# Two expert layers around a state-space mixer: first-pass results scattered plainly to two row arrays and summed by VectorE in the mixer

## The reference

```
x = x + 0.5 * ffn(layernorm(x), Wg, W11, W12, W2)
x = x + mixer(layernorm(x))
x = x + 0.5 * ffn(layernorm(x), Wg, W11, W12, W2)

ffn(x):   s = softmax(x @ Wg)                  # 8 experts
          top 2 of s, their scores divided by their sum
          y_e = (silu(x @ W11[e]) * (x @ W12[e])) @ W2[e]      # 256 -> 512 -> 256
          out = sum over the two chosen e of score_e * y_e
mixer(T): Tn = T / rms(T) * norm_scale;  x, z = split(Tn @ in_w.T + in_b)
          x = pointwise(depthwise conv of 3 taps(x))
          y = (ssm forward(x) + ssm backward(x)) * sigmoid(z)  # h = h*a + u*b, 64 states each
          out = T + y @ out_w.T + out_b
```

## Time and profile before

| | us |
|---|---|
| median of 3 runs | 1028.68 (1026.73 to 1032.29) |
| the profiled execution | 1028.27, span 1026.4 |
| TensorE busy | 914.3 (89%) |
| VectorE busy | 591.1 (58%) |
| ScalarE busy | 340.2 (33%) |
| GpSimd busy | 607.3 (59%) |

### The profile page before, as it was taken

One profiled execution on the slowest core, in us unless ns is written; L12 is line 12 of the kernel. 1 busy time (PEld: TensorE's weight loads), 2 busy tenths in 40 slices (PEclk: granted clock), 3 DMA queues, 4 the chain that ended last, 5 costly groups with the idle time before them and its releaser, 6 DMA issues.

```text
span 1026.4 us, 20394 instructions
## 1 busy us (share of the span) xinstructions
PE 914.3 (89%) x5386; PEld 780.3 (76%) x5390; DVE 591.1 (58%) x1447; ACT 340.2 (33%) x699; POOL 607.3 (59%) x549
## 2 busy tenths in 40 slices
PE   7658899999999899976997994699999999999995
PEld 7647787878878788864774773478888888888884
DVE  3765565556656565546766875855555555555552
ACT  5743342333423333311327531023322332233221
POOL 3415666767667677734305760167777777777673
PEclk9969999999999999998999995699999999999999
DMA  9576547365363654323212548133344333433332
GB/s 315 195 264 187 150 89 195 77 168 160 79 188 73 179 131 95 49 32 103 63 41 86 186 156 347 45 71 77 53 74 77 56 72 53 79 76 52 52 50 30
DMA packets 78275, 116.06 MB, mean 113 GB/s; under 512 B 12048, under 2 KB 61072, under 8 KB 77904
## 3 DMA queue, kind: packets, MB, share of 16 engines
q0 software_dynamic: 31808, 37.83, 23.1%
q1 hardware_dynamic: 32896, 51.92, 14.8%
q10 hardware_dynamic: 13520, 25.70, 7.3%
HBM read 70.99 MB, written 48.63 MB: 117 GB/s over the span
## 4 chain that ended last, share of the span: by engine, by line
PE 60%; DVE 11%; issue 8%; POOL 6%; ACT 5%; DMA 4%; ACTq 3%; SPq 2%; POOLq 0%; another core or an unknown queue 0%; DVEq 0%
PE bank L1412 32%; PE bank L1435 16%; PE bank L1421 5%; PE bank L1404 3%; POOL seq L466 2%; PE bank L1533 2%; DVE work L834 2%; DMA xg<-xn_rows,idx_i 1%; SPq L306 1%; DVE sg L1078 1%; ACTq L648 1%; DVE bnst L822 1%; ACTq L646 1%; DVE w_lo L1143 1%; ACT sg L657 1%
## 5 line engine op out<-in xcount | busy, mean ns | idle before, releaser
L1078 DVE TENSOR_TENSOR sg<-sg,bank 128x512 f32<-128x512 f32 x142 | 97.7, 688 | 309.0 <-ACT sg L657 256.9
L1412 PE MATMUL bank<-w_hi,xt_hi 128*128 x568 | 241.3, 425 | 25.3 <-DVE xt_lo L1067 19.0
L1412 PE MATMUL bank<-w_hi,xt_lo 128*128 x568 | 224.6, 395 | 0.0
L1412 PE MATMUL bank<-w_lo,xt_hi 128*128 x568 | 222.8, 392 | 0.0
L649 ACT ACTIVATE yb<-bank,gates_in 128x256 f32<-128x256 f32 x142 | 67.4, 475 | 454.1 <-issue 234.0
L477 POOL DMA_INDIRECT xg<-xn_rows,idx_i x142 | 142.6, 1004 | 98.4 <-DVE idx_i L921 55.8
L481 POOL DMA_INDIRECT gates_in<-gate_rows,idx_g x142 | 138.6, 976 | 55.3 <-issue 42.3
L1435 PE MATMUL bank<-w_hi,ft_hi 128*128 x568 | 160.0, 282 | 7.7 <-ACT yb L649 7.7
L490 POOL DMA_INDIRECT x_rows<-yb,idx_i x71 | 116.5, 1641 | 82.5 <-ACT yb L649 30.5
L1435 PE MATMUL bank<-w_hi,ft_lo 128*128 x568 | 160.5, 283 | 0.0
L1435 PE MATMUL bank<-w_lo,ft_hi 128*128 x568 | 159.0, 280 | 0.0
(11 more groups left out here) (250 smaller groups left out, 1251.5 us busy)
## 6 DMA issues: line engine op xcount, KB each, us to landing
xn_rows<-work SPq DMA_DIRECT2D x16, 512.0 KB, 3.0
w_lo_rows<-w_lo ACTq DMA_DIRECT2D x16, 512.0 KB
w_lo<-w_lo_rows SPq DMA_DIRECT2D x16, 512.0 KB
work<-x_rows SPq DMA_DIRECT2D x16, 512.0 KB, 3.8
w_lo<-w_lo_rows SPq DMA_DIRECT2D x2, 4096.0 KB, 17.5
x_all<-x SPq DMA_DIRECT2D x8, 512.0 KB, 9.3
w_lo_rows<-in_sb ACTq DMA_DIRECT2D x16, 256.0 KB
out_rows<-seq SPq DMA_DIRECT2D x8, 512.0 KB, 3.3
```

Source lines behind the costliest of these rows:

```text
L1078: nc.vector.tensor_tensor(sg[p], sg[p], ps_g[p][:], ALU.mult).then_inc(f_step, 1)
L1412: last = nc.tensor.matmul(dst[p][:], xt[p][:, c, :], of(w), start=(c == 0 and n == 0), stop=(c == DC - 1 and n == len(parts) - 1))
```

## The change

The first pass no longer adds its results to a copy of x. Its index has one number per pair: first choices go to rows 0 to 4095 of a new array `y_rows`, second choices to rows 4096 to 8191, pads behind, by a plain scatter. The mixer loads x and both halves of y per chunk, VectorE adds them, and SP stores the sum to `x1_rows`. `norm_x1` moves from VectorE to ScalarE. SP, not ScalarE, loads the weights (a slot at a time, W2 directly into the place of its high part, from where ScalarE copies it to a stage) and stores the low parts of W11 and W12. The rounding of weights is cut into halves, one per tile. `apply_x` of chunks 0 to 3 moves to VectorE, with three buffers. GpSimd gathers six tiles' rows before the third gate gather. In the backward half the residual x + layernorm(x) is one ScalarE operation per tile, (1+rstd)*x - mean*rstd.

```
 SP, router:
-            for dram in (xn_dram, x1_dram, out):
+            for dram in (xn_dram, out):
...
-                sp.wait_ge(norm_ready, k + 1)
-                sp.dma_start(rows(xn_dram, k), xn[k % 2]).then_inc(xn_out[k % 2], 16)
-            sp.dma_start(x1_dram[0:L, :].rearrange(...), x.rearrange(...)).then_inc(x1_out, 16)
+                sp.dma_start(rows(xn_dram, k), xn_x[k % 3]).then_inc(xn_x_out[k % 3], 16)
 SP, first pass (a new order; load_slot loads w11, w12, then w2 of slot j):
             store_gates(0)
-            load_w2_lo(0)
+            load_w2_lo(0, 0)
+            def load_ahead(j, tile):
+                sp.wait_ge(ye_done, tile + 1)
+                load_slot(sp, j)
+            load_ahead(1, 1)
+            store_up_lo(0)
+            load_ahead(2, 5)
+            load_w2_lo(0, 1)
+            load_ahead(3, 9)
+            store_up_lo(1)
+            load_ahead(4, 13)
...
 SP, mixer:
-            sp.wait_ge(added, 16 * ET)
-            for b in range(2):
-                sp.dma_start(xin[b], rows(x1_dram, b)).then_inc(x_in[b], 16)
...
+            for p in range(2):
+                sp.wait_ge(y_out[p], 16 * ((ET + 1 - p) // 2))
+            sp.wait_ge(lo_out, 32 * E)
+            load_x1(0, 0)
+            load_y(0)
+            load_x1(1, 1)
+            for i in range(NCH):
+                b = i % 2
+                sp.wait_ge(summed, i + 1)
+                if i + 1 < NCH:
+                    load_y(i + 1)
+                sp.dma_start(rows(x1_dram, i), xin[b]).then_inc(x1_out[b], 16)
+                if i + 2 < NCH:
+                    sp.wait_ge(norm_ready, i + 1)
+                    sp.wait_ge(x1_out[b], 16 * (i // 2 + 1))
+                    load_x1(i + 2, b)
 GpSimd, experts:
+                    if r == 0:
+                        nc.gpsimd.indirect_dma_start(y_dram, bass.IndirectOffsetOnAxis(ap=idx_s[:, t:t + 1], axis=0), yb[t % 2], None).then_inc(y_out[t % 2], 16)
+                        return
...
-                for t in range(XG):
+                for t in range(XG + 1):
                     gather(t)
                 pool.wait_ge(gates_out, 16 * (r + 1))
                 for t in range(XG):
                     gather_gates(t)
+                    if t == 1:
+                        gather(XG + 1)
 GpSimd, residual:
-                nc.gpsimd.tensor_tensor(x2[b], xin[b], t_rows[b], ALU.add).then_inc(res_step, 1)
-                nc.gpsimd.tensor_tensor(x2[b], x2[b], outb_sb[:]..., ALU.add).then_inc(res_ready, 1)
+                nc.gpsimd.tensor_tensor(x2[b], t_rows[b], outb_sb[:]..., ALU.add).then_inc(res_ready, 1)
 ScalarE, weights:
+            def high_down(j, h):
+                at_ = w2_hi[:, j * IC + 2 * h:j * IC + 2 * h + 2, :].rearrange("p c d -> p (c d)")
+                act.wait_ge(w2_in, 16 * (j + 1))
+                if j > 0:
+                    act.wait_ge(w2_lo_out, 16 * j)
+                nc.scalar.activation(w2_stage[h], at_.bitcast(F32), ACT.Copy).then_inc(staged, 1)
+                act.wait_ge(staged, 2 * j + h + 1)
+                nc.scalar.activation(at_, w2_stage[h], ACT.Copy).then_inc(hi2_ready, 1)
 in weights_step:
+                    if s in (1, 2):
+                        high_down(j, s - 1)
                     if s == 4:
                         store_low(j)            # now one DMA, of w2's low part
+                    if s in (3, 4):
+                        high_up(j, s - 3)
+                    if s in (5, 6):
+                        high_value(j, s - 5)
 ScalarE, router:
-                if k > 0:
-                    apply_x(k - 1, (k - 1) % 2)
-            apply_x(NCH - 1, (NCH - 1) % 2)
+                if k > NCH // 2:
+                    apply_x(k - 1)              # apply_x(7) follows the first one-hot product
 ScalarE, mixer:
+            def norm_x1(i, b):
+                act.wait_ge(rstd_ready, i + (NCH + 1))
+                if not (isinstance(i, int) and i < 2):
+                    act.wait_ge(tr_done, i - 1)
+                for t in range(G):
+                    last = nc.scalar.activation(xn[b][:, t, :], xin[b][:, t, :], ACT.Identity, scale=rstd[:, b, 1, t:t + 1], bias=rstd[:, b, 0, t:t + 1])
+                last.then_inc(norm_ready, 1)
             for i in range(2):
-                rows_high(i, i)
+                norm_x1(i, i)
+            rows_high(0, 0)
+            rows_high(1, 1)
+            norm_x1(2, 0)
             gate_out(0)
-            with act.Fori(0, NCH // 2 - 1) as j:
+            norm_x1(3, 1)
+            with act.Fori(0, NCH // 2 - 2) as j:
                 for b in range(2):
                     rows_high(j * 2 + (b + 2), b)
                     gate_out(j * 2 + (b + 1))
+                    norm_x1(j * 2 + (b + 4), b)
 VectorE, router, after top2_x(k):
+                if 3 <= k < 7:
+                    apply_x(k - 3)
 VectorE, mixer:
             def stats_x1(i, m, b):
                 dve.wait_ge(x_in[b], m * 16 + 16)
+                dve.wait_ge(y_in, i * 32 + 32)
+                flat = xin[b].rearrange("p t d -> p (t d)")
+                nc.vector.tensor_tensor(flat, flat, y_in_sb[0], ALU.add).then_inc(half_sum, 1)
+                dve.wait_ge(half_sum, i + 1)
+                nc.vector.tensor_tensor(flat, flat, y_in_sb[1], ALU.add).then_inc(summed, 1)
+                dve.wait_ge(summed, i + 1)
                 ln_stats(i + NCH, b, rows_of(b))
...
             with dve.Fori(0, NCH // 2 - 2) as j:
                 for b in range(2):
                     c = j * 2 + b
-                    norm_x1(j * 2 + (b + 3), 1 - b)
                     take_u(c, b)
                     rows_low(j * 2 + (b + 2), b)
                     scan_forward(c)
                     stats_x1(j * 2 + (b + 4), j + 2, b)
```

More of the change, by code:

```diff
@@ new lines, in _ @@
+            load_ahead(1, 1)
[5 more added lines that the diff above has]
+            load_ahead(4, 13)
+            load_w2_lo(0, 2)
+            store_up_lo(2)
+            load_ahead(5, 16)
+            load_ahead(6, 19)
+            load_ahead(7, 22)
+            for j in range(3, E):
+                load_w2_lo(0, j)
+                store_up_lo(j)
+            sp.wait_ge(w2_lo_in, E * 16)
@@ L518, in _ @@
             experts(0)
-            with pool.Fori(0, NCH // 2) as j:
-                for b in range(2):
-                    rsqrt_rms(j * 2 + b, b)
+            for i in range(NCH):
+                rsqrt_rms(i, i % 2)
             pool.wait_ge(s_attw, 64)
@@ L573, in high_value @@
+            def high_value(j, c):
                 act.wait_ge(w12_in, 16 * (j + 1))
[L574 to L581 removed]
@@ L626, in tiles_by_p @@
                     nc.scalar.activation(pair_tile_x[g % 2][:, 0], at_tile[g % 2], ACT.Copy, scale=p_plus_1[:]).then_inc(by_p_ready, 1)
+                    if g == 0:
+                        apply_x(NCH - 1)
+                    if g == NQB - 1:
+                        act.wait_ge(xn_x_out[2], 16 * (NCH // 3))
                     if g > 0:
-                        (high_up, high_value, high_down)[g - 1](0)
+                        for c in range(2):
+                            (high_up, high_value, high_down)[g - 1](0, c)
             def experts(r):
@@ L729, in _ @@
                     gate_out(j * 2 + (b + 1))
+                    norm_x1(j * 2 + (b + 4), b)
+            for i in range(NCH - 2, NCH):
+                rows_high(i, i % 2)
+                gate_out(i - 1)
             gate_out(NCH - 1)
@@ L828, in ln_stats, with apply_x @@
                 last.then_inc(mv_ready, 1)
+            def apply_x(k):
+                dve.wait_ge(rstd_ready, k + 1)
+                if k >= 3:
+                    dve.wait_ge(xn_x_out[k % 3], 16 * (k // 3))
+                for t in range(k * G, (k + 1) * G):
+                    last = nc.vector.tensor_scalar(xn_x[k % 3][:, t % G, :], x_all[:, t, :], x1_rstd[:, t:t + 1], x1_mean[:, t:t + 1], ALU.mult, ALU.add)
+                last.then_inc(norm_dve, 1)
             def ln_apply(k, b, src, which=0):
@@ L1095, in experts @@
                     nc.vector.tensor_copy(v(UB), ps_w[:, D:D + 1]).then_inc(wct_ready, 1)
-                    low_down(0)
+                    for h in range(2):
+                        low_down(0, h)
                     gates(0)
@@ L1199, in _ @@
                 stats_x1(b, 0, b)
-            for b in range(2):
-                norm_x1(b, b)
             dve.wait_ge(m_ready, 1)
@@ L1205, in _ @@
             stats_x1(2, 1, 0)
-            norm_x1(2, 0)
             rows_low(1, 1)
```

316 lines of the change are left out of this document (162 added, 154 removed).

## The result

The changed kernel took 1092.19 us (median; 1091.62 to 1092.79), the kernel before beside it 1029.18 (1026.73 to 1032.29): ratio 1.0611 [1.0581, 1.064], slower. The profiled execution took 1091.62 with a span of 1089.9. The forecast was 1053, range 1033 to 1067: the direction was right, the size outside the range.

| stage | before | after | difference | forecast |
|---|---|---|---|---|
| to the first up product | 73.2 | 66.7 | -6.5 | -6.5 |
| first pass, to the last down product | 381.8 | 418.0 | **+36.2** | +1 (+11.5 -10.5) |
| to the last gate product of the mixer | 88.2 | 121.1 | +32.9 | +33 |
| to the last logits product | 81.6 | 78.6 | -3.0 | -3 |
| router, to the next up product | 37.3 | 38.5 | +1.2 | +0.6 |

A forecast was written before the change was run, and what follows sets the result against it. TensorE was taken as full in the second pass, with 22.3 us of waits in the first and VectorE the mixer's old forward ring; -6.5 +11.5 -10.5 +33 -3 +0.6 = +25.1 on 1028.3 gives 1053 us, range 1033 to 1067.

The forecast's parts named there:

- Router: Before the first pass: apply_x split 2.8 us earlier, no x copy under first gather -2.8, faster clock -0.9; together -6.5.
- A stall at the first tiles: First pass, ahead of tile 3: slot 1's weights wait for down(0), so ScalarE's w2 copies hold up TensorE; +11.5 us.
- Rival (b): First tiles: no stall at slot 1, data there when ScalarE asks; -11.5, total 1041.5 us; chance 12%.
- Steady tiles of slots 1 to 7: First pass: ScalarE loses DMA issues, halves its rounding and gains staging copies, so TensorE waits less; -10.5 us.
- Rival (c): First pass: experts gain nothing, as two dependent copies stand where DMA issues stood; +10.5, total 1064 us; chance 12%.
- Into the mixer: Hand-over to the mixer: more loads, VectorE adds and ScalarE's norm delay the ramp; +17.3 us, part of the +33.
- the mixer's loop: Mixer's forward half: serial ring through ScalarE's queue, 12.6 us per chunk instead of 8.53, four turns +16.3, part of +33.
- Rival (a): Mixer hides its new work: loop stays 8.1 to 8.5 us; +3 instead of +33, total 1023; chance 8%.
- (d): Mixer loop: TensorE falls to 1.2 GHz, needing 16 us per chunk; +17, total 1070; chance 8%.
- Backward half: Mixer's backward half: norm_t and residual lose operations, TensorE stops the turn at about 8.3 us; -3.
- indices(1): Second router: three more operations of 0.24 us on the path; +0.6.
- sign of its failure: Forecast counted as wrong if a forward chunk is near 8.5 us or first-pass TensorE waits beyond tile 3 stay at 20.

The follow-up runs named there:

- late-copy kernel: Changed kernel with accumulating scatters, old mixer forward half and old weight handling, x copied in one piece behind the last xn store: 1024.84 us, ratio 0.9949 to before.
- batch A: One chip: value steps early 1.0272, slot 1's weights ordered at once 1.0429, ScalarE's mixer order turned 1.0371, all three edits 1.0089, ratios to the kernel before.
- value steps early: Changed kernel with both w12 high halves in step 5 and both low halves in step 6: 1051.41 us, ratio 1.0272 (batch A); 1076.32, 1.0476 (batch D).
- batch E: One chip: y arrays with old weight handling 1037.85 us; all three edits 1033.82; all three edits with each scatter waiting for the last 1032.87.
- batch C: One chip, no y arrays: new weight handling with x copied in pieces 1025.09 us; old handling, copy in pieces 1019.59; old handling, copy late 1024.84.
- order in the mixer: Changed kernel with ScalarE's norm_x1 one chunk later in its queue, so rows_high(c+3) precedes norm_x1(c+4): 1061.75 us, ratio 1.0371.
- batch B: One chip: changed kernel 1093.77 us; TensorE's wait for w12's low half moved later 1081.82; all three edits plus ramp edits 1058.56; no y arrays 1036.01.
- batch D: One chip: changed kernel 1092.53 us; value steps early 1076.32; all three edits 1062.39; no y arrays, old weight handling, x copied in pieces 1020.34.
- all three edits: Changed kernel with value steps early, slot 1's weights ordered at once and ScalarE's mixer order turned: ratio 1.0089 (batch A), 1.031 (batch D), 1.0069 (batch E).
- the old weights without y arrays: Changed kernel with accumulating scatters, old mixer forward half, old weight handling and x copied in pieces: 1020.34 us, ratio 0.9916 in batch D.
- the new weights without y arrays: Changed kernel with value steps early and slot 1 at once, but accumulating scatters and the old mixer forward half: 1036.01 us, ratio 1.0055 in batch B.
- the ramp's kernel: All three edits plus two pairs of y buffers, loads two chunks ahead, and rows_high(0) ahead of norm_x1(1): 1058.56 us, ratio 1.0286.
- The two orderings together: Value steps early and slot 1's weights ordered at once, measured within all three edits: first pass 422.0 to 399.1 us in batch D.

## Why the prediction was wrong

- *Router, -6.5*: right in size (first up product 66.69; before 73.23), by three terms of which one is right. GpSimd starts the first gather 4.0 us earlier, not 2.8 (61.51 against 65.50). TensorE has its rows 3.1 instead of 5.8 us later, without the copy beside it: -2.7, as forecast. The late-copy kernel shows that the first half is worth nothing without the second. The 0.9 for the clock lie behind the first up product and were not gained: after the wait at 72.07 the matmuls take 0.63 all the same.
- *A stall at the first tiles, +11.5*: right in place and size, 12.1 and a restart at 0.63 per matmul. Rival (b) fell. The data come from SP's first order in 7.8 us, where the forecast had 6.4.
- *Steady tiles of slots 1 to 7, -10.5*: **the step that failed.** I added up ScalarE's extras per tile and never set the new last step of VectorE against TensorE's wait at the head of the turn. low_value(j, 1) went from step 5 to step 7, so each of seven slots is waited for: 21.0 us of waits on record, 18.0 in batch A, down to 0.4 there with the value steps early. Measured in place of -10.5: 36.2 - 12.1 = +24.1. That is 21.0 at the heads of the turns and 9.4 of longer busy time (the restart at slot 1 among it), less 6.3, since the rest of TensorE's idle time is 19.1 against 25.4. The tally itself was not tested alone: without the waits at the heads the profiled first pass is 7.5 us shorter than with the old handling where both have y arrays (batch E), with accumulating scatters it is the same and the total 5.5 us longer (batch C). Rival (c), no gain in the experts, had the place but neither the cause nor the size. How much of the +24.1 would be left on another chip is open; the edit of the value steps alone gives back 17.0 to 22.8.
- *Into the mixer* and *the mixer's loop, +33*: +32.9. The first `ssm_in` product comes 41.9 us behind the last down product instead of 27.0 (+14.9; forecast 15), and four turns of 12.4 instead of 8.5 are +15.6 (forecast 16.3). The mechanism of the turn is shown by turning the order round. Rival (a) fell. So did (d), though the clock did fall (0.84 over the stretch; the eight transposes take 1.97 us at 546.70, in the turn shown, and 1.09 at 559.00, 571.45 and 583.75): the turns are 12.4 us with either, so TensorE's work was not the bound. The additions took 1.19 to 1.23 us with GpSimd idle, as forecast. The rule of the Trainium skill ("SBUF — State Buffer", "Who interferes with whom") on two SBUF inputs beside GpSimd was not put to the test by them.
- *Backward half, -3*: -3.0, but not as worked out. TensorE was said to stop the turn at about 8.3; from the third chunk on the turns are 7.8 long, and TensorE is busy throughout (7.78 of 7.78 us from 643.78), and some of the old ones were already 7.8. That the sum came out is in part luck. *indices(1), +0.6*: +1.2. The second pass's +2.7 was not forecast.

The forecast named the sign of its failure: "a first pass whose TensorE waits beyond tile 3 stay at 20 us". They rose to 38.

## What stays open

On the run on record and in batches B and D the first pass of kernels with y arrays takes 17 to 27 us more than in batches A and E. ScalarE's ft_hi then starts late, and the profile names no releaser ("remote"). One case in the changed kernel, the transposes of fu and the ft_hi that needs them alone:

```profile
152.90 0.60 PE L1521 MATMUL bank<-ident,fu 128*128 128x128 f32 x4
...
157.29 0.60 ACT L704 ACTIVATE ft_hi<-bank 128x512 fp32r<-128x512 f32 x1 [3.81 <-remote]
```

The trace's record of semaphores says a little more: in this case and in five of the other seven of over 1 us, ft_hi starts 0.02 us behind the update that the transposes' end should give, and that update stands 2.4 to 3.9 us behind their end (as the profile models it). There it is the signal that comes late, and ScalarE starts at once.

And ft_hi from 100 to 430 us (busy, mean ns | idle before), for all three edits in batch D, the same in batch A, the old weights without y arrays in batch D, and the new weights without y arrays in batch B:

```profile
L705 ACT ACTIVATE ft_hi<-bank 128x512 fp32r<-128x512 f32 x60 | 35.8, 597 | 33.8 <-remote 27.6 <-PE bank L1524 6.1
```
```profile
L705 ACT ACTIVATE ft_hi<-bank 128x512 fp32r<-128x512 f32 x66 | 39.4, 597 | 0.4
```
```profile
L659 ACT ACTIVATE ft_hi<-bank 128x512 fp32r<-128x512 f32 x63 | 37.7, 598 | 0.4
```
```profile
L680 ACT ACTIVATE ft_hi<-bank 128x512 fp32r<-128x512 f32 x61 | 36.4, 597 | 3.9 <-PE bank L1468 2.4 <-remote 1.2
```

So it takes both the batch's chip and a kernel with y arrays: on the chip of batch B the new handling of the weights shows 1.2 us of it without y arrays and 16.2 with them (the ramp's kernel). Whether the new handling is needed too was not settled, nor what brings it. Each chip stood in one batch only, so chip and hour can't be told apart, and that the late starts are what lengthens the pass by 17 to 27 us is likely, not shown. The two orderings together give back 23 us where they occur (batch D, first pass 422.0), and 29 in batch A, where it is 401.1.

## What to carry to other kernels

When work is spread evenly over steps, look for who waits for the last piece: a consumer that asks once per turn feels only the last step. Here it came two steps later and cost 21 us of waits; one step earlier gave 17 to 23 us back, more than the 7.5 that all the spreading gained at best. In an in-order queue put what depends on the furthest-ahead data last; ScalarE's norm of the chunk furthest ahead, one place too early in its queue, cost 10 us. And before crediting an edit with a gain at a stage's start, check which transfer lies under that stage: the 4 MB copy, moved to where the DMA engines were half busy (0.51 of their time from 27 to 44 us in the kernel before), brought 5 us with no other change.

## What the runs showed of the hardware

ft_hi took 596 to 598 ns (mean from 100 to 430 us) in all five batches, while the first pass of one and the same kernel took 371.8 us on two chips and 399.1 on a third; the second pass took 363 to 369 in every run. A single edit is therefore judged beside a control on its own chip, not against the run on record. The granted clock fell to 1.2 GHz behind a wait of 2.36 us at the head of a turn (batch A, order in the mixer, at 297.63) and not behind one of 2.83 at another head (changed kernel, at 217.00): the length of the wait alone did not decide it.
